# Eight products of sequence 0 ahead of the pipeline, and the scalings at the turn to the experts between the links of two chains

## The reference, cut to what matters

```python
x = x + attn(xn, Wqkv, Wo, ...) + ffn(xn, ...)          # xn = layernorm(x), x: (32, 256, 128) float32
# attn: 16 heads of 8 features, rotary angles, decay bias, causal softmax
# ffn:
n1 = layernorm(xn); rw = gating(n1)                     # 8 experts, at least 2 active
q = einsum('btc,ech,bte->bth', n1, q_proj, rw)          # the same with k_proj, v_proj
attn_out = einsum('bth,ehc,bte->btc', softmax(q @ k.T) @ v, o_proj, rw)
hs = xn + attn_out
n2 = layernorm(hs); rw2 = gating(n2)
inter = gelu(einsum('btc,eci->btei', n2, w1))           # 8 experts again
out = hs + einsum('btei,eic,bte->btc', inter, w2, rw2)
```

## Time and profile before

| | us |
|---|---|
| median of 3 runs | 1212.77 |
| lowest, highest run | 1212.22, 1213.09 |
| the profiled execution's own time | 1212.19 |
| its span | 1210.4 |
| busy: TensorE | 1161.8 |
| busy: VectorE | 1018.8 |
| busy: ScalarE | 717.7 |
| busy: GpSimd | 245.9 |

### The profile page before, as it was taken

One profiled execution on the slowest core, in us unless ns is written; L12 is line 12 of the kernel. 1 busy time (PEld: TensorE's weight loads), 2 busy tenths in 40 slices (PEclk: granted clock), 3 DMA queues, 4 the chain that ended last, 5 costly groups with the idle time before them and its releaser, 6 DMA issues.

```text
span 1210.4 us, 33207 instructions
## 1 busy us (share of the span) xinstructions
PE 1161.8 (96%) x10652; PEld 896.3 (74%) x10652; DVE 1018.8 (84%) x3687; ACT 717.7 (59%) x1292; POOL 245.9 (20%) x374
## 2 busy tenths in 40 slices
PE   2599999999999999999999999999999999999998
PEld 1377777778777788777777777777877667777776
DVE  8889999999999999999999998999876577777664
ACT  5166666666666656666666666666557745555532
POOL 5222222222222232222222222223322000000000
PEclk9989999999999999999999999999999999999999
DMA  4443233333323333233333323333331234444453
GB/s 109 129 125 91 90 94 106 104 108 89 94 93 91 90 94 91 94 92 89 94 106 107 103 90 93 92 91 91 95 93 54 96 151 165 174 176 168 172 189 120
DMA packets 103113, 133.01 MB, mean 110 GB/s; under 512 B 13576, under 2 KB 82424, under 8 KB 94864
## 3 DMA queue, kind: packets, MB, share of 16 engines
q1 hardware_dynamic: 100548, 130.72, 34.6%
q10 hardware_dynamic: 2508, 1.58, 0.5%
HBM read 109.12 MB, written 21.54 MB: 108 GB/s over the span
## 4 chain that ended last, share of the span: by engine, by line
PE 77%; DVE 14%; issue 6%; ACT 1%; ACTq 1%; DVEq 1%; DMA 1%; POOL 0%; SPq 0%; POOLq 0%
PE ps L1621 10%; PE ps L1667 10%; PE ps L1898 9%; PE ps L1622 9%; PE ps L1884 9%; PE ps L1631 5%; PE ps L1494 3%; PE ps L1598 3%; PE ps L1581 2%; PE ps L1557 2%; PE ps L1547 2%; PE ps L1544 2%; DVE att L1249 1%; PE ps L1554 1%; PE ps L1603 1%
## 5 line engine op out<-in xcount | busy, mean ns | idle before, releaser
L1223 DVE TENSOR_REDUCE mx<-ps 128x4 f32<-128x1024 f32 (+1 forms) x192 | 234.8, 1223 | 35.8 <-PE ps L1557 20.7
L789 ACT ACTIVATE pr<-ps 128x1024 f32<-128x1024 f32 x192 | 196.7, 1024 | 77.1 <-PE ps L1581 54.3
L637 POOL TENSOR_TENSOR n1s<-rep,n1T 128x256 f32<-128x256 f32 x256 | 177.3, 731 | 297.8 <-DVE mpart L1237 280.7
L795 ACT ACTIVATE ps<-trn 128x1024 f32<-128x1024 bf16 x191 | 196.5, 1029 | 5.1
L1898 PEld LDWEIGHTS ps<-w2s,ats 128*128 128x128 f32 x1024 | 131.4, 191 | 53.4 <-issue 43.9
L1621 PE MATMUL ps<-n1s,wqk 128*128 128x256 f32 x512 | 164.7, 404 | 1.3 <-issue 1.3
L1622 PE MATMUL ps<-n1s,wqk 128*128 128x256 f32 x512 | 153.8, 382 | 0.0
L989 ACT ACTIVATE n1s<-ps 128x512 f32<-128x512 f32 x128 | 76.6, 598 | 121.3 <-PE ps L1884 120.2
L1898 PE MATMUL ps<-w2s,ats 128*128 128x128 f32 x1024 | 136.1, 276 | 2.9 <-DVE ats L1422 2.8
L1631 PE MATMUL ps<-wv,n1s 128*128 128x128 f32 x1024 | 133.1, 278 | 0.0
L1884 PE MATMUL ps<-rep,w1s 128*128 128x512 f32 x256 | 130.7, 594 | 0.0
(11 more groups left out here) (229 smaller groups left out, 2051.4 us busy)
## 6 DMA issues: line engine op xcount, KB each, us to landing
rep<-scr_rw SPq DMA_DIRECT2D x32, 1024.0 KB, 5.6
stk<-scr_rw SPq DMA_DIRECT2D x16, 1024.0 KB, 8.2
scr_parts<-parts SPq DMA_DIRECT2D x64, 192.0 KB, 5.8
stk<-scr_parts SPq DMA_DIRECT2D x248, 48.0 KB
rots<-scr_rw SPq DMA_DIRECT2D x8, 1024.0 KB, 4.8
wqk<-scr_rw SPq DMA_DIRECT2D x8, 1024.0 KB, 8.7
stk<-scr_parts SPq DMA_DIRECT2D x248, 32.0 KB
xt<-in_x SPq DMA_DIRECT2D x32, 128.0 KB, 2.1
```

Of the source, the lines that this page charges most:

```text
L637: pool.tensor_tensor(n1s[:, e], rep[:, par, e], n1T[:, par], ALU.mult).then_inc(n1s_done, 1)
L789: act.activation(pr[:, Q, :, i], ps[:, S2[0]:S2[0] + NF], ACT.Exp).then_inc(exp_done, 1)
L795: act.activation(ps[:, S2[0]:S2[0] + NF], seeds[:, kind:kind + 1].broadcast_to((P, NF, 512)), ACT.Copy).then_inc(seed_done, 1)
L1223: dve.tensor_reduce(mx[:, min(i, 1)].rearrange("p (f h) -> p f h", f=NF)[:, :, h:h + n], ps[:, S1[0]:S1[0] + NF].rearrange("p f (h t) -> p ...
```

## The change

It has two parts. In the first, `qk(0, 4)` and `qk(0, 5)` go in front of the transposition of the maxima (`max_T(0)`), `qk(0, 6)` between `norm_T(2)` and `proj(2)`, and `qk(0, 7)` behind `proj(2)`; step 0 then has none. The wait of TensorE for the stored gate weights of sequence 1 (`rwT_done`) goes behind the first `unit1` and `unit2` of step 0. In the second, at the turn, the scalings of units 3 and 4 go into LN2's chain and behind its end, those of units 5 to 9 behind links 4, 9, 14, 19 and 24 of the gating.

```diff
@@ -59,6 +59,7 @@
+GELU_FIRST = (4, 9, 14, 19, 24)
 GELU_AT = (2, 7, 12, 17, 22, 27)
@@ -1439,13 +1440,17 @@
                     norm = layer_norm2(2)
-                    for _ in range(6):
-                        next(norm, None)
-                    scale_gelu(a, 2)
-                    run(norm)
+                    for k, more in enumerate((6, 5, 13)):
+                        for _ in range(more):
+                            next(norm, None)
+                        scale_gelu(a, 2 + k)
+
+                early = ((a, 5), (a, 6), (a, 7), (b, 0), (b, 1))
 
                 def beside_gating(k):
-                    if k in GELU_AT[(g == 0):]:
+                    if g == 0 and k in GELU_FIRST:
+                        scale_gelu(*early[GELU_FIRST.index(k)])
+                    elif g and k in GELU_AT:
                         scale_gelu(a, 2 + GELU_AT.index(k))
@@ -1455,7 +1460,8 @@
                 for e in range(E):
-                    scale_gelu(b, e)
+                    if g or e >= 2:
+                        scale_gelu(b, e)
                     if e == 1:
                         finish(a)
@@ -1741,6 +1747,8 @@
                 next_max(0)
                 unit2(n, u, 0)
+                if isinstance(n, int) and n == 0:
+                    pe.wait_ge(rwT_done, 2)
                 first_qk(0)
...
-                qk(n, 4)
+                first_qk(4)
...
-                qk(n, 5)
+                first_qk(5)
...
-                qk(n, 6)
+                first_qk(6)
...
-                qk(n, 7)
+                first_qk(7)
@@ -1851,11 +1859,14 @@
             qk(0, 2)
             qk(0, 3)
+            qk(0, 4)
+            qk(0, 5)
             max_T(0)
             norm_T(2, LATER, lambda: pe.wait_ge(s1_read, UNITS))
+            qk(0, 6)
             proj(2, LATER, lambda: None)
+            qk(0, 7)
             weights_T(1, lambda: pe.wait_ge(rwT_done, 1))
-            pe.wait_ge(rwT_done, 2)
```

## The result

| | before | after |
|---|---|---|
| median of 7 runs, us | 1212.69 | 1216.86 |
| lowest, highest | 1212.05, 1213.09 | 1215.48, 1218.53 |
| ratio, 95% interval | | 1.0036 [1.0025, 1.0047] |
| the profiled execution, its span | 1212.19, 1210.4 | 1218.53, 1216.7 |

The account below looks back on a forecast made before the run. TensorE was taken to bound the steps from the second on and the experts from down(10), VectorE most of step 0 and the turn; -1.0 + 2.65 + 1.8 = +3.45 us gave 1216.2, 8-in-10 range 1213.0 to 1218.2.

Parts of the forecast that it names:

- The turn, +2.65: At the turn, VectorE waits for ScalarE's gelus, so unit 10's scaling comes later and down(10) starts 2.65 us later.
- The two waits: At the turn, VectorE waits for gelu 4 ahead of unit 4's scaling, 1.5 us, and gelu 7 ahead of unit 7's, 1.4.
- the ceiling of 0.2 us: At the turn, the most to gain, since VectorE is busy nearly throughout between its third and eleventh scaling: 0.2 us.
- The clock, +1.8: Clock halves after TensorE's 4.4 us gap ahead of down(10): 1.8 us by the nearest row, 3.2 by a longer half-rate stretch.
- Step 0, -1.0: In step 0, moved products shorten VectorE's waits for TensorE, but the clock falls there: gain 1.0 us, bounds 0 to 1.9.
- the maximum at 70.94: In step 0, VectorE's maximum after a 1.47 us wait for TensorE was to start 1.2 us earlier.
- the maximum at 77.62: In step 0, VectorE's later maximum, after a 0.36 us wait for TensorE, was to come only 1.0 us earlier.
- (a): Rival: turn as forecast, but the clock stays full through step 0, gaining 1.9 there; +2.55, 1215.3 us; chance 0.12.
- (b): Rival: the turn costs its 2.65 us but the clock does not fall; 1213.5 to 1214.4 us; chance 0.28.
- (c): Rival: at the turn VectorE's waits at units 4 and 7 are hidden; -3.4, 1209.4 us; chance 0.06.
- (d): Rival: all 5.3 us of TensorE's work come out of step 0, against 2.65 at the turn; 1210.1 us; chance 0.03.
- (e): Rival: no prologue gain, a product delays max_T(0) or the projection; forecast plus 1.0, 1217.2 us; chance 0.04.

Follow-up runs that it names:

- e3: The changed kernel with ScalarE's gelu 4 ahead of all norms of tile 4 and gelu 7 ahead of the tanh: 1215.35 us, 1.0020 against before.
- e1: The changed kernel with the prologue's part undone, so the turn's part alone: 1216.93 us, 1.0033 against before.
- e5: The kernel before with only unit 3's scaling moved into LN2's chain: 1212.48 us, 0.9999 against before.
- e7: The turn's part alone, plus gelus 4, 5 and 7 earlier, TensorE's transposition of tile 4 one unit later, and e9's edit: 1208.55 us, 0.9967 against before.
- e9: The kernel before with finish(0) and the LN2 of pair 3 moved behind unit 10's scaling: 1211.37 us, 0.9994 against before.
- e4: The changed kernel with four unread products in TensorE's long wait ahead of down(10): 1214.72 us, 1.0018 against before.
- e2: The changed kernel with the turn's part undone, so the prologue's part alone: 1213.04 us, 1.0005 against before.
- e6: e2 with eight unread matmul pairs in TensorE's waits of step 0: 1211.37 us, 0.9991 against before.
- e8: e6's prologue part with step 0 filled, together with e7's replanned turn: 1207.44 us, 0.9958 against before.

## Why the prediction was right, point by point

**The turn, +2.65.** Measured +2.54. The two waits were put at 1.5 and 1.4 and are 1.43 and 1.31, at the places named and with the releaser named; TensorE's wait ahead of `down(10)` was put at about 3.9 with 0.1 of work in 4.4, and is 3.57 with 0.30 in 3.87. e3 shows the cause by taking both waits away, e1 that this part is the whole loss. e5, with no gain, agrees with the ceiling of 0.2 us; e7 and e9 pass it only because they take work out of the stretch.

**The clock, +1.8.** It fell where forecast. The rest took 2.45 more in after, 1.43 more in e1, 2.9 in e3 and nothing in e4. By the medians it is 2.1 (after against e4). The row chosen gave 1.8; the traces lie on both sides of it and all below the other, 3.2. In the rows of that price, from 45.27 on, before's granted clock reads 1.00, and the half rate shows only in the durations; e9's trace has the same durations at 45.24 (1.19 and 1.06 us) with a granted clock of 0.50, so the reading holds. The rule of the Trainium skill named there, that the clock falls after a sustained idle stretch ("TensorE: Matmul & The Clock Gate", section "Part 1: The HAM clock gate"), agrees with the fall in the gap of 3.57 us. With step 0's fall in after, where no wait was over 1.73 us, and with the falls in the 2.19 us wait of e2 and e6 it does not agree; there the measurement decides.

**Step 0, -1.0: the term that was mis-sized.** Most steps held: no product delayed the maxima or the projection measurably, the clock stayed full through the prologue's end (1.00 in 52.90 to 57.20) and fell inside step 0, the maximum at 70.94 came 1.19 us earlier counted from the rotation (forecast 1.2), `pv(0)` took 2.7 us until the next slot (forecast 2.9). What failed is the next step, that the maximum at 77.62 would be 1.0 earlier: counted the same way it is 1.17 earlier in e2 and 1.21 in e4, 0.6 in e3, and 0.08 later in after, where the half level lasted to 75.70. The forecast also took one trace as the standard, and one in which the clock rose late; step 0 of before's code takes 24.50 on average, 0.3 less than in that trace, and in e5 the first of the two maxima came 1.04 earlier with the old code. Mean against mean, the first is 0.9 us earlier in the four changed traces than in the six old ones, the second 0.4. So the term is -0.4 by the means. e2's time shows no gain at all (+0.4, from -0.5 to +1.7); its trace gains 1.16 us in step 0 against before's and loses 0.78 at the turn.

**The sum.** The order and the prologue's part cost +2.1 together, against 2.65 - 1.0 = 1.65, and the clock +2.1, against 1.8; the sum is +4.2, against 3.45. The total does not bear out the -1.0, for without it the forecast would have been 1217.2, nearer to the measured 1216.86 than 1216.2 is.

**The rivals.** (a), the clock full through step 0, falls with the half level from 62.10. (b), no fall at the turn, falls with [1.0025, 1.0047] and the window behind 992.11; e4, which makes its case on purpose, comes at +2.1. (c), the waits hidden, falls with the two waits; it is what e7 needed three further edits to reach. (d), 5.3 us out of step 0, falls with e2. (e), nothing from the prologue, gave 1217.2 and cannot be told from the forecast by the time. Its mechanism, a delay of the maxima or the projection, does not show; its outcome for that part is nearer than mine.

## What to carry to other kernels

Where two engines work through written orders that wait for each other, a scaling moved forward on one must be checked against what the other has queued in front of its operand; the wait filled here was not on the path, and the two made by filling it were. A wait closed early is worth only as much as the last wait before the saturated stretch moves, so both ends are to be moved together (e5 alone 0, e9 alone about -0.8, e7 -4.1). And idle time collected into one long gap just ahead of such a stretch cost a second time by the clock here; a few unread products in it gave back 2.1 us. Where a stretch is thin enough for the clock to fall in it, its duration in one trace is that of one position of the fall, and two kernels are compared over several traces.

## What the runs showed of the hardware

The granted clock fell in two ways that I had not expected. The same wait of 2.19 us left it full in before and was followed by half clock in e2 and in e6, for a cost of 0.8 us; what differs is not known (both have the changed prologue and the old turn, but so small a number decides nothing). And the fall in or ahead of step 0 came later with more work ahead of it, at 61.1 to 63.6 in five traces (after, e2, e3, e4, e6) against 55.5 to 57.9 in five of the six with the old prologue; but in e5, the sixth, it came at 61.1 as well, so the code alone does not set the moment. With the same code the rise again lay 7.8 to 10.2 us behind the rotation, and step 0 took 23.74 to 24.88 with it. The fall was seen avoided in one trace only, e8; with the same additions it fell in e6, so that too may be the execution and not the code. The start of the program varies by about 1 us between executions with the same code (rotation at 59.20 to 60.20), which is as much as the terms argued over here: a stretch is to be measured from its own start, and over several traces.
